# Attention of a decoder layer: heads packed on tiles of the TensorE array, weighted values one group later

## Chip, cores and metric

One core of a Trainium2 chip runs the whole kernel in one launch. The metric is the device time of that launch in microseconds (us). Three runs of the kernel before gave 1297.28, 1297.92 and 1300.14 us; their median is 1297.92 us.

## What is computed

The kernel is one decoder layer with B = 8 sequences of L = 100 tokens and D = 256 features: a two-way Mamba mixer, cross attention to a context of S = 361 tokens, and a mixture of experts. The change is in the cross attention, which is, for every sequence:

```python
q, k, v = heads(x2n @ Wq), heads(ctx @ Wk), heads(ctx @ Wv)   # H = 16 heads of HD = 16 features
p = softmax(q @ k.T / sqrt(HD))        # 100 x 361 for each head
x = x + concat(p @ v) @ Wo + bo
```

All of it is float32. Products of which the operands would be rounded are made of three: high x high, high x low, low x high part.

## The kernel before

Five instruction streams (PE is TensorE, DVE is VectorE, ACT is ScalarE, POOL is GpSimd, SP issues DMAs) run in orders written out by hand and meet at semaphores. The stages follow one another: the mixer (up to about 778 us in the trace), norms and a fusing product, the attention (about 829 to 1060 us), the experts.

In the attention the loop runs over the 8 sequences, and within a sequence over 8 groups of two heads. For group g of sequence b:

- `scores(b, r, g)`, PE: 2 heads x 3 matmuls (through the helper `three`, L1011), each with 128 rows of contraction, 100 columns of stationary queries and 362 moving key columns. So that 128 features can be contracted for a head of 16, POOL spreads the queries (`spread_queries`, L666): in `q_blk` each head has a copy of the 128 features in which all but its own 16 are zero. The scores of a group go to banks 0 and 1, or 2 and 3, of PSUM.
- `maxima`, DVE: the row maxima of both heads (L1626), and their product with -1/sqrt(HD), the tile `shift` (L1629).
- `exponentials`, ACT: two exponentials (L901), each of which also sums its row into `mass` (a second record, ACTIVATION_READ_ACCUMULATOR).
- `turn_probs`, PE: 6 transposes (L1170) into banks 4 and 5. `copy_probs` copies one bank on DVE (L1637) and the other on ACT (L910).
- `weigh_values`, PE: 2 heads x 3 matmuls, where the probabilities are stationary (100 columns) and the 16 value columns of the head move (L1186). The trace has a float32 matmul as two records, so twelve here; a float32r matmul (scores, keys, values) and a transpose are one.

PE's order in `attend` is, for g from 2: `turn_probs(g)`, `scores(g + 2)`, a piece of the next sequence's keys or values (keys with g = 2 and 3, values with g = 4 and 5), `weigh_values(g)`. ACT takes `copy_probs(g)`, `exponentials(g + 2)` and, with g = 2 and 3, the high part of the keys (`high_keys`, L892). DVE takes `copy_probs(g)`, `maxima(g + 2)`, the low part of the keys (`low_keys`, L1613) or the copy of the values. At the end of a sequence DVE divides by the mass (`normalise_heads`), PE transposes the 100x256 result (`turn_heads`), DVE copies it, and PE multiplies with Wo (`project_heads`, 2 matmuls); DVE adds that to `x_tok` (`add_attention`, L1659). Keys, values and the heads' result share the bank KEY_BANK.

Of the kernel before, what the change touches and what calls it, by code (L numbers as in the profile page):

```python
# [18 lines left out]
F32 = mybir.dt.float32  # L19
# [8 lines left out]
P = 128  # L28
B, L, D = 8, 100, 256
T = B * L  # L30
# [52 lines left out]
KEY_BANK = 7  # L83
# [75 lines left out]
def decoder_layer(nc, x, ctxT, winT, wxT, wdtT, woutT, vec, ln_g, ln_b, wfuseT, bfuse,  # L159
                  wqT, wkT, wvT, woT, bo, wg, w1, b1, w2, b2, out):  # L160
    stack = ExitStack()
    with stack:
# [3 lines left out]
        def sem(name):  # L166
# [7 lines left out]
        head_mask = sb("head_mask", [P, HT])  # L174
        one = sb("one", [P, 1])
# [55 lines left out]
        qT_part = [sb(f"qT_{n}", [P, KD, T], F32R, scope=attn) for n in "hl"]  # L231
        q_blk = [[sb(f"q_blk_{n}{r}", [P, KD, HT, L], F32R, scope=attn) for n in "hl"] for r in range(2)]
        ctx_sb = [sb(f"ctx{r}", [P, KD, S], scope=attn) for r in range(2)]
        ctx_part = [[sb(f"ctx_{n}{r}", [P, KD, SE], F32R, scope=attn) for n in "hl"] for r in range(2)]
        wq_sb, wk_sb, wv_sb, wo_sb = (sb(n, [P, KD, D], scope=attn) for n in ("wq_sb", "wk_sb", "wv_sb", "wo_sb"))
        wk_part, wv_part = ([sb(f"{w}_{n}", [P, KD, D], F32R, scope=attn) for n in "hl"] for w in ("wk", "wv"))
        kT_part = [[sb(f"kT_{n}{r}", [P, KD, SE], F32R, scope=attn) for n in "hl"] for r in range(2)]
        v_sb = [sb(f"v{r}", [P, KT, D], scope=attn) for r in range(2)]
        probs = [sb(f"probs{r}", [L, 2, KT * P], scope=attn) for r in range(2)]
        probsT = [[sb(f"probsT{r}{j}", [P, KT * L], scope=attn) for j in range(2)] for r in range(2)]  # L240
        neg_max, shift, mass, inv_mass = (
            sb(n, [L, 2, H], scope=attn) for n in ("neg_max", "shift", "mass", "inv_mass"))
        heads_tok = sb("heads_tok", [L, D], scope=attn)
        headsT = sb("headsT", [P, KD, L], scope=attn)
# [118 lines left out]
        q_blk_ready = sem("q_blk_ready")  # L363
# [10 lines left out]
        shift_ready = sem("shift_ready")  # L374
# [6 lines left out]
        headsT_done = sem("headsT_done")  # L381
# [34 lines left out]
        def tile(k):  # L416
            return slice(k * P, (k + 1) * P)

# [13 lines left out]
        def _(sp):  # L432
# [120 lines left out]
        def _(pool):  # L553
# [21 lines left out]
            fill(head_mask[:], 1.0)  # L575
# [73 lines left out]
            pool.wait_ge(attnw_in, 16 * 4)  # L649
# [10 lines left out]
            def spread_queries(b, r):  # L660

                for m in range(KD):
                    if isinstance(b, int):
                        job_copied(pool, ("qT", m, b // BQ))
                    for part, block in zip(qT_part, q_blk[r]):
                        nc.gpsimd.tensor_tensor(  # L666
                            block[:, m],
                            part[:, m, bass.ds(b * L, L)].bitcast(F32).unsqueeze(1).broadcast_to([P, HT, L]),
# [1218 lines left out]
```

## Time and profile before

| | |
|---|---|
| median of three runs | 1297.92 us |
| the profiled execution | 1293.94 us |
| its span on the core | 1292.2 us |
| PE, DVE, ACT, POOL busy | 80%, 72%, 42%, 61% of the span |
| granted TensorE clock, mean | 0.914 of full speed |
| attention, from the first transposed probabilities to the last add | 846.58 to 1060.27 us |

Busy times are sums of records; matmuls are pipelined, so their records overlap, and the time that one costs is the distance between two starts.

### The profile page before, as it was taken

The numbers are of one execution on the slowest core, as the hardware profiler recorded it, in microseconds if no ns is written. First come the engines' busy times: TensorE is split into PE (matmuls) and PEld (weight loads), VectorE is DVE, ScalarE is ACT, GpSimd is POOL, SyncE is SP. The second block draws the span as 40 slices with busy tenths as digits, with TensorE's granted clock in tenths as the row PEclk, the third lists the DMA queues.
The fourth block names the chain that finished last, engine by engine and source line by source line (L and its number), as shares of the span: only waits on it lengthen the run. The fifth ranks groups of instructions, "written<-read, shape, count | busy, mean of one in ns | idle before, by whom it ended". The sixth has DMA issues, their size and how long they took to land.

```text
span 1292.2 us, 14793 instructions
## 1 busy us (share of the span) xinstructions
PE 1033.0 (80%) x4832; PEld 705.2 (55%) x4832; DVE 925.3 (72%) x1068; ACT 542.0 (42%) x1188; POOL 782.5 (61%) x469
## 2 busy tenths in 40 slices
PE   7596676767667676676765779889999979899996
PEld 5243333433334333343332447779999966499995
DVE  6978998998989989999999993666666652021111
ACT  2686443443444434444444431244444433133231
POOL 4255998998998989989899890555223000402112
PEclk9877888998979989799898999999999988899998
DMA  5001344454544434344454430331000000959995
GB/s 163 1 7 45 98 103 105 94 111 87 110 105 90 108 89 110 105 93 104 94 111 105 96 83 7 115 113 36 13 0 0 0 1 1 331 170 303 319 311 142
DMA packets 95706, 131.70 MB, mean 102 GB/s; under 512 B 12153, under 2 KB 89098, under 8 KB 95626
## 3 DMA queue, kind: packets, MB, share of 16 engines
q1 hardware_dynamic: 91738, 126.59, 36.7%
q0 software_dynamic: 3904, 4.33, 1.8%
q8 instruction: 31, 0.51, 0.2%
q14 instruction: 33, 0.27, 0.1%
HBM read 122.48 MB, written 9.23 MB: 102 GB/s over the span
## 4 chain that ended last, share of the span: by engine, by line
PE 37%; DVE 27%; issue 26%; POOL 5%; ACT 1%; SPq 1%; another core or an unknown queue 1%; DMA 1%; DVEq 0%; POOLq 0%; ACTq 0%
DVE states L1538 13%; DVE states L1550 10%; PE ps L1011 6%; PE ps L1378 6%; PE ps L1392 5%; PE ps L1186 4%; PE ps L1004 3%; PE ps L1170 2%; PE ps L1078 2%; PE ps L1069 2%; PE ps L1315 2%; PE ps L1324 2%; POOL dt L596 1%; POOL dtu L600 1%; POOL row_sel L565 1%
## 5 line engine op out<-in xcount | busy, mean ns | idle before, releaser
L619 POOL TENSOR_TENSOR states<-states,c_row 128x800 f32<-128x800 f32 x255 | 474.4, 1883 | 58.7 <-DVE states L1550 57.7
L1550 DVE TENSOR_TENSOR_SCAN states<-ps,states 128x800 f32<-128x800 f32 x256 | 462.7, 1830 | 0.0
L852 ACT ACTIVATE ps<-dt,neg_a 128x396 f32<-128x396 f32 x512 | 283.4, 585 | 361.8 <-DVE states L1550 361.8
L1078 PE MATMUL ps<-states,ident 128*128 128x400 f32 x1024 | 417.1, 543 | 1.9 <-POOL states L619 1.9
L1078 PEld LDWEIGHTS ps<-states,ident 128*128 128x128 f32 x1024 | 211.2, 210 | 142.0 <-issue 52.4
L1538 DVE TENSOR_TENSOR states<-dtu,ps 128x800 f32<-128x800 f32 x192 | 188.1, 980 | 31.1 <-PE ps L1060 28.3
L1060 PE MATMUL ps<-b_parts,row_sel 96*128 96x400 bf16 x192 | 69.0, 360 | 161.8 <-DVE states L1538 156.3
L1060 PEld LDWEIGHTS ps<-b_parts,row_sel 96*128 96x128 bf16 x192 | 18.9, 99 | 237.6 <-DVE states L1538 220.1
L610 POOL TENSOR_TENSOR states<-dtu,b_row 128x800 f32<-128x800 f32 x64 | 121.1, 1892 | 0.0
L901 ACT ACTIVATE probs<-ps,shift 100x361 f32<-100x361 f32 x128 | 70.8, 559 | 99.1 <-DVE shift L1629 99.1
L740 POOL DMA_INDIRECT sums<-y_tile,x_tile x20 | 30.9, 1546 | 133.7 <-DMA sums<-y_tile,x_tile 92.6
L971 ACT ACTIVATE hid_tile<-ps,w_tile 128x128 f32<-128x128 f32 x160 | 45.6, 368 | 97.8 <-PE ps L1378 97.8
L1186 PEld LDWEIGHTS ps<-v,probsT 128*100 128x100 f32 (+1 forms) x768 | 75.4, 168 | 10.9 <-issue 8.3
L666 POOL TENSOR_TENSOR q_blk_h<-qT_h,head_mask 128x800 fp32r<-128x800 f32 x16 | 24.4, 1524 | 91.2 <-PE ps L1011 81.4
L1186 PE MATMUL ps<-v,probsT 128*100 128x16 f32 (+1 forms) x768 | 74.9, 236 | 5.4 <-ACT probsT L910 4.6
L1378 PEld LDWEIGHTS ps<-x_turned,w_tile 128*128 128x128 f32 x640 | 75.4, 194 | 2.2 <-issue 1.3
L1378 PE MATMUL ps<-x_turned,w_tile 128*128 128x128 f32 x640 | 75.7, 277 | 1.0 <-DVE out_tok L1789 1.0
L1626 DVE TENSOR_REDUCE neg_max<-ps 100x2 f32<-100x722 f32 x64 | 58.1, 908 | 25.5 <-PE ps L1011 25.5
L731 POOL DMA_INDIRECT rows_by_slot<-rows_src,slot_idx x16 | 16.0, 1000 | 99.7 <-DVE slot_idx L1765 95.1
L1392 PE MATMUL ps<-w_tile,hid_tile 128*128 128x256 f32 x320 | 72.2, 379 | 0.0
L1392 PEld LDWEIGHTS ps<-w_tile,hid_tile 128*128 128x128 f32 x320 | 59.3, 190 | 7.3
L994 PE MATMUL ps<-xT,win 128*128 128x400 f32 x128 | 52.8, 579 | 7.4 <-ACT u_pad L753 7.4
(220 smaller groups left out, 1326.4 us busy)
## 6 DMA issues: line engine op xcount, KB each, us to landing
c_row<-rows SPq DMA_DIRECT2D x256, 200.0 KB, 3.1
w_tile<-in_w SPq DMA_DIRECT2D x40, 1024.0 KB, 5.1
b_row<-rows SPq DMA_DIRECT2D x64, 200.0 KB, 4.1
ctx<-in_ctxT SPq DMA_DIRECT2D x8, 361.0 KB, 4.3
rows_by_slot<-blank_rows SPq DMA_DIRECT2D x1, 2660.0 KB, 11.6
x_tile<-rows_by_slot SPq DMA_DIRECT2D x20, 133.0 KB, 3.4
win<-in_winT SPq DMA_DIRECT2D x2, 1024.0 KB, 9.4
w_shared<-in_w SPq DMA_DIRECT2D x2, 1024.0 KB, 6.6
```

The costliest lines, as they stand in the source:

```text
L610: nc.gpsimd.tensor_tensor(states[i % RING][:].rearrange("p (c t) -> p c t", c=CP), dtu[d][:, cp * CP:(cp + 1) * CP, chunk(q)], b_row[turn ...
L619: nc.gpsimd.tensor_tensor(st, st, c_row[i % C_SLOTS][:].unsqueeze(1).broadcast_to([P, CP, TQ]), ALU.mult).then_inc(product_ready, 1)
L852: nc.scalar.activation(seqs(decay[i % DECAYS][:, j * TQ:(j + 1) * TQ])[:, :, 1:], seqs(dt_sb[d][:, c, chunk(q)])[:, :, 1:], ACT.Exp, scale ...
L901: nc.scalar.activation(probs[g % 2][:, j, 0:S], ps[0:L, g % 2 * 2 + j, 0:S], ACT.Exp, bias=shift[:, r, h:h + 1], scale=HD ** -0.5, accum_o ...
L1011: mm = nc.tensor.matmul(to, w[i], x[j], start=(first and n == 0), stop=(last and n == 2))
L1060: nc.tensor.matmul(ps[:, 6 + turn % 2, 0:TQ], row_sel[:, n, :], b_parts[d][:, chunk(q)], start=True, stop=True).then_inc(b_bank_ready, 1)
L1078: mm = nc.tensor.matmul(ps[:, j, 0:TQ], ident[:], states[i % RING][:, j * TQ:(j + 1) * TQ], start=False, stop=(i % N == N - 1), skip_group ...
L1186: mm = nc.tensor.matmul(ps[0:L, 6, h * HD:(h + 1) * HD], probsT[g % 2][j][0:size, kt * L:(kt + 1) * L], v_sb[r][0:size, kt, h * HD:(h + 1) ...
L1378: mm = nc.tensor.matmul(ps[:, hid_bank(k, ft), ft % 4 * P:(ft % 4 + 1) * P], w[:, W1_AT + m * F + ft * P:W1_AT + m * F + (ft + 1) * P], x_ ...
L1392: mm = nc.tensor.matmul(ps[:, 6 + k % 2, 0:D], hid_tile[k % 2][:, ft, :], w[:, W2_AT + ft * D:W2_AT + (ft + 1) * D], start=(ft == 0), stop ...
L1538: nc.vector.tensor_tensor(states[i % RING][:].rearrange("p (c t) -> p c t", c=CP), dtu[d][:, cp * CP:(cp + 1) * CP, chunk(q)], ps[:, bank_ ...
L1550: nc.vector.tensor_tensor_scan(st, decay[i % DECAYS], st, 0.0, ALU.mult, ALU.add).then_inc(scan_done, 1)
```

## The change

Only the attention changes. (1) The 16 features of a head are assigned to a strip of 32 rows of the array (two heads share a strip; a mask keeps only one of them, in `q_part[par]`, and has the factor 1/sqrt(HD) in it). A score matmul contracts 32 rows, and the two heads of a group lie in neighbouring strips, issued in turn. POOL's spreading of the queries is gone; ACT and DVE make two masked copies of the queries instead of one. (2) The value matmuls are turned around: the values of a head, 16 columns, a column of ones and 15 zeros, are stationary (32 columns), the 100 columns of transposed probabilities move, and the results of the two heads go to neighbouring strips of 32 PSUM partitions. The column of ones gives the mass of each row. (3) So ACT no longer sums, DVE no longer makes `shift`, and the 128 x 400 result needs no transpose; a matmul with a selecting matrix spreads the mass, DVE takes the reciprocal of 128 x 400 elements and multiplies, and Wo is applied by 4 matmuls instead of 2, from a `wo_sb` that 8 small DMAs fill. (4) `weigh_values` is issued one group later. (5) PE's loop over the sequences is written out; POOL zeroes the padded tiles before the attention.

```diff
-            fill(head_mask[:], 1.0)
+            fill(head_mask[:], HD ** -0.5)
...
-            for w_dram, w_sbuf in ((wqT, wq_sb), (wkT, wk_sb), (wvT, wv_sb), (woT, wo_sb)):
+            for w_dram, w_sbuf in ((wqT, wq_sb), (wkT, wk_sb), (wvT, wv_sb)):
...
+            sp.wait_ge(wo_zeroed, 1)
+            for m in range(KD):
+                for j in range(P // QUAD):
+                    sp.dma_start(wo_sb[j * QUAD:j * QUAD + HD, m * PAR:(m + 1) * PAR, :],
+                                 woT.rearrange("(m j r i) e -> m j i r e", m=KD, j=P // QUAD, r=PAR)[m, j]
+                                 ).then_inc(wo_in, 16)
...
+            job_result(pool, ("mix", DIRS - 1, B // 2 - 1))
+            nc.gpsimd.memset(wo_sb[:], 0.0).then_inc(wo_zeroed, 1)
+            nc.gpsimd.memset(mass_sel[:], 0.0).then_inc(sel_ready, 1)
+            for r in range(2):
+                nc.gpsimd.memset(v_sb[r][:], 0.0).then_inc(v_zeroed, 1)
...
-            spread_queries(0, 0)
...
-            spread_queries(1, 1)
...
             def high_queries(m, q):
                 job_result(act, ("qT", m, q))
-                nc.scalar.activation(qT_part[0][:, m, chunk(q)], bank(("qT", m, q))[:, 0:TQ], ACT.Copy
-                                     ).then_inc(q_high, 1)
+                for i in range(PAR):
+                    ins = nc.scalar.activation(q_part[i][0][:, m, chunk(q)], bank(("qT", m, q))[:, 0:TQ],
+                                               ACT.Identity, scale=par_mask[:, i:i + 1])
+                ins.then_inc(q_high, 1)
...
                     nc.scalar.activation(probs[g % 2][:, j, 0:S], ps[0:L, g % 2 * 2 + j, 0:S], ACT.Exp,
-                                         bias=shift[:, r, h:h + 1], scale=HD ** -0.5,
-                                         accum_out=mass[:, r, h:h + 1]).then_inc(probs_ready, 1)
+                                         bias=neg_max[:, r, h:h + 1]).then_inc(probs_ready, 1)
...
-                for j in range(2):
-                    mm = three(ps[0:L, g % 2 * 2 + j, 0:SE], [part[:, m, (2 * g + j) % HT, :] for part in q_blk[r]],
-                               [part[:, m, :] for part in kT_part[r]], True, True)
+                for n, (hi, lo) in enumerate(((0, 0), (0, 1), (1, 0))):
+                    for i in range(2):
+                        _, j, par = head_at(2 * g + i)
+                        rows = slice(j * QUAD, (j + 1) * QUAD)
+                        mm = nc.tensor.matmul(ps[0:L, g % 2 * 2 + i, 0:SE],
+                                              q_part[par][hi][rows, m, b * L:(b + 1) * L],
+                                              kT_part[r][lo][rows, m, :], start=(n == 0), stop=(n == 2))
...
-                for j in range(2):
-                    h = 2 * g + j
-                    for kt in range(KT):
-                        size = P if kt < KT - 1 else SL
-                        mm = nc.tensor.matmul(ps[0:L, 6, h * HD:(h + 1) * HD],
-                                              probsT[g % 2][j][0:size, kt * L:(kt + 1) * L],
-                                              v_sb[r][0:size, kt, h * HD:(h + 1) * HD],
+                for kt in range(KT):
+                    size = P if kt < KT - 1 else SL
+                    for i in range(2):
+                        m, j, par = head_at(2 * g + i)
+                        block = (2 * g + i) // (P // QUAD)
+                        mm = nc.tensor.matmul(ps[j * QUAD:(j + 1) * QUAD, HEAD_BANK, block * L:(block + 1) * L],
+                                              v_sb[r][0:size, kt, m * HT + j * PAR + par, :],
+                                              probsT[g % 2][i][0:size, kt * L:(kt + 1) * L],
                                               start=(kt == 0), stop=(kt == KT - 1))
...
-            def turn_heads(b):
+            def spread_mass(b):
                 pe.wait_ge(heads_ready, b + 1)
...
+                nc.tensor.matmul(ps[:, KEY_BANK, 0:BLOCKS * L], mass_sel[:], heads_raw[:].rearrange("p k t -> p (k t)"),
+                                 start=True, stop=True).then_inc(mass_spread, 1)
...
+                for k in range(BLOCKS):
+                    mm = nc.tensor.matmul(ps[0:L, KEY_BANK, 0:D], headsT[:, k, :], wo_sb[:, k, :], start=(k == 0),
+                                          stop=(k == BLOCKS - 1))
...
-                    weigh_values(b, r, g)
+                    weigh_values(b, r, g - 1)
                 if last:
-                    turn_heads(b)
+                    weigh_values(b, r, GROUPS - 1)
+                    spread_mass(b)
                     project_heads(b)
                 else:
                     turn_probs(b + 1, 0)
                     scores(*nxt, 2)
-                    turn_heads(b)
-                    weigh_values(*nxt, 0)
+                    weigh_values(b, r, GROUPS - 1)
                     turn_probs(b + 1, 1)
                     scores(*nxt, 3)
+                    spread_mass(b)
+                    weigh_values(*nxt, 0)
                     project_heads(b)
-                    weigh_values(*nxt, 1)
...
-            with pe.Fori(0, B // 2 - 1) as i:
-                attend(2 * i + 1, 1)
-                attend(2 * i + 2, 0)
+            for b in range(1, B - 1):
+                attend(b, b % 2)
...
                 nc.vector.tensor_reduce(neg_max[:, r, 2 * g:2 * g + 2], ps[0:L, g % 2 * 2:g % 2 * 2 + 2, 0:S],
-                                        AX.X, ALU.max).then_inc(max_ready, 1)
-                dve.wait_ge(max_ready, GROUPS * b + (g + 1))
-                nc.vector.tensor_scalar(shift[:, r, 2 * g:2 * g + 2], neg_max[:, r, 2 * g:2 * g + 2],
-                                        -HD ** -0.5, None, ALU.mult).then_inc(shift_ready, 1)
+                                        AX.X, ALU.max, negate=True).then_inc(max_ready, 1)
...
+            def copy_heads(b):
+                dve.wait_ge(pv_done, GROUPS * b + GROUPS)
+                nc.vector.tensor_copy(heads_raw[:].rearrange("p k t -> p (k t)"), ps[:, HEAD_BANK, 0:BLOCKS * L]
+                                      ).then_inc(heads_ready, 1)
+
+            def normalise_heads(b):
+                dve.wait_ge(mass_spread, b + 1)
+                nc.vector.reciprocal(inv_mass[:].rearrange("p k t -> p (k t)"), ps[:, KEY_BANK, 0:BLOCKS * L]
+                                     ).then_inc(inv_mass_ready, 1)
                 dve.wait_ge(inv_mass_ready, b + 1)
...
+                nc.vector.tensor_tensor(headsT[:], heads_raw[:], inv_mass[:], ALU.mult).then_inc(headsT_copied, 1)
...
-                normalise_heads(b, r)
                 if not last:
                     copy_probs(b + 1, 0)
                     maxima(b + 1, 1 - r, 2)
                 copy_heads(b)
-                if last:
-                    norm_x(0, rows_src)
                 if not last:
                     copy_probs(b + 1, 1)
                     maxima(b + 1, 1 - r, 3)
+                normalise_heads(b)
+                if last:
+                    norm_x(0, rows_src)
                 add_attention(b)
```

## Rows read from the trace of the kernel before

**Rows 1.** Windows: stretch, length, busy (count) of PE, PEld, DVE, ACT, POOL, clock, DMA, GB/s.
```profile
933.40:1038.67 105.27, 103.83 (x914) 99.78 (x913) 64.28 (x128) 52.11 (x168) 23.81 (x16) 1.00 0.00 0
1038.67:1060.27 21.60, 16.80 (x134) 14.36 (x133) 11.85 (x32) 8.35 (x24) 0.00 (x0) 0.84 0.00 1
```

**Rows 2.** Timeline, a group of the last sequence without keys or values: start, length, engine, operation.
```profile
1043.50 0.71 PE L1170 MATMUL ps<-ident,probs 100*128 100x100 f32 x6
...
1043.99 0.39 PE L1011 MATMUL ps<-kT_h,q_blk_h 128*100 128x362 f32 x1
...
1044.25 0.47 DVE L1637 COPY probsT<-ps 128x300 f32<-128x300 f32 x1 [0.96 <-PE ps L1170]
...
1044.41 0.42 ACT L910 ACTIVATE probsT<-ps 128x300 f32<-128x300 f32 x1
...
1044.88 0.32 PE L1011 MATMUL ps<-kT_h,q_blk_l 128*100 128x362 f32 x1
1045.04 1.15 PE L1186 MATMUL ps<-v,probsT 128*100 128x16 f32 x12
1045.24 0.91 DVE L1626 TENSOR_REDUCE neg_max<-ps 100x2 f32<-100x722 f32 x1 [0.52 <-PE ps L1011]
1046.04 0.71 PE L1170 MATMUL ps<-ident,probs 100*128 100x100 f32 x6
...
1046.39 0.56 ACT L901 ACTIVATE probs<-ps,shift 100x361 f32<-100x361 f32 x1 [1.56 <-DVE shift L1629]
...
1047.48 0.42 ACT L910 ACTIVATE probsT<-ps 128x300 f32<-128x300 f32 x1
...
1062.47 0.88 ACT L753 ACTIVATE xn3T<-ps 128x400 f32<-128x400 f32 x2
```

**Rows 3.** Timeline, a group with keys (g = 3) and the values that follow.
```profile
911.07 0.46 DVE L1637 COPY probsT<-ps 128x300 f32<-128x300 f32 x1
911.45 0.90 DVE L1626 TENSOR_REDUCE neg_max<-ps 100x2 f32<-100x722 f32 x1
...
912.59 0.56 ACT L901 ACTIVATE probs<-ps,shift 100x361 f32<-100x361 f32 x1 [1.65 <-DVE shift L1629]
...
913.68 0.47 ACT L892 ACTIVATE kT_h<-ps 128x362 fp32r<-128x362 f32 x1
...
914.18 0.53 DVE L1613 TENSOR_TENSOR kT_l<-ps,kT_h 128x362 fp32r<-128x362 f32 x1 [1.62 <-ACT kT_h L892]
...
914.63 0.46 DVE L1637 COPY probsT<-ps 128x300 f32<-128x300 f32 x1
...
914.86 0.29 PE L1011 MATMUL ps<-wv_h,ctx_h 128*128 128x256 f32 x1
...
916.29 1.15 PE L1186 MATMUL ps<-v,probsT 128*100 128x16 f32 x12
```

**Rows 4.** Timeline, PE alone: 8 float32 matmuls with 9 stationary and 100 moving columns.
```profile
1109.59 1.54 PE L1302 MATMUL ps<-ident,rows_src 100*9 100x100 f32 x16
```

**Rows 5.** Groups of DVE instructions, shapes apart: busy us, mean ns.
```profile
L1641 DVE RECIPROCAL inv_mass<-mass 100x16 f32<-100x16 f32 x8 | 1.9, 243 | 0.0
L1445 DVE RECIPROCAL rstd<-std 100x4 f32<-100x4 f32 x10 | 1.8, 178 | 7.7 <-ACT std L749 7.7
...
L1456 DVE COPY xn2T<-ps 128x400 f32<-128x400 f32 x2 | 1.0, 564 | 0.0
```

**Rows 6.** Timeline, the start of the attention.
```profile
839.95 3.66 DVE L1629 TENSOR_SCALAR shift<-neg_max 100x2 f32<-100x2 f32 x1
...
846.58 0.70 PE L1170 MATMUL ps<-ident,probs 100*128 100x100 f32 x6 [3.18 <-DVE qT_l L1604]
...
853.39 0.47 DVE L1637 COPY probsT<-ps 128x300 f32<-128x300 f32 x1 [1.42 <-PE ps L1170]
```

**Rows 7.** Windows of one microsecond, columns as in rows 1.
```profile
845.00:846.00 1.00, 0.00 (x0) 0.00 (x0) 0.73 (x2) 0.63 (x2) 1.00 (x2) 1.00 0.00 0
...
1054.00:1055.00 1.00, 0.55 (x4) 0.44 (x3) 0.34 (x1) 0.10 (x1) 0.00 (x0) 0.50 0.00 0
```

More of the change, by code:

```diff
@@ L82 @@
 ROUTE_CONSTS = 13
-KEY_BANK = 7
+KEY_BANK, HEAD_BANK = 7, 6
+QUAD = 32
+PAR = QUAD // HD
+BLOCKS = H // (P // QUAD)
+HEAD_CONSTS = 7
 FIRST_KEYS, FIRST_VALUES = (0, 1), (4, 5)
@@ L417, in tile, with head_at @@
             return slice(k * P, (k + 1) * P)
+        def head_at(pos):
+            m, rest = divmod(pos, HT)
+            par, j = divmod(rest, P // QUAD)
+            return m, j, par
         def hid_bank(k, ft):
@@ L647, in split_context @@
                 split_into([part[:, :, 0:S] for part in ctx_part[r]], ctx_sb[r][:], ctx_split, 2 * b)
-            pool.wait_ge(attnw_in, 16 * 4)
+            job_result(pool, ("mix", DIRS - 1, B // 2 - 1))
[3 more added lines that the diff above has]
+                nc.gpsimd.memset(v_sb[r][:], 0.0).then_inc(v_zeroed, 1)
+            pool.wait_ge(sel_ready, 1)
+            selected = mass_sel[:].rearrange("p (j i) -> p j i", i=QUAD)
+            nc.gpsimd.affine_select(out=selected, in_=selected, compare_op=ALU.not_equal, fill=1.0, base=-HD,
+                                    pattern=[[-QUAD, P // QUAD], [0, QUAD]], channel_multiplier=1
+                                    ).then_inc(sel_ready, 1)
+            pool.wait_ge(v_zeroed, 2)
+            for r in range(2):
+                nc.gpsimd.memset(v_sb[r][:, :, :, HD:HD + 1], 1.0).then_inc(v_zeroed, 1)
+            pool.wait_ge(attnw_in, 16 * 3)
             for n, (part, raw) in enumerate(((wk_part, wk_sb), (wv_part, wv_sb))):
@@ L659, in _ @@
                 nc.gpsimd.memset(probs[r][:, :, S:], 0.0).then_inc(probs_zeroed, 1)
[L660 to L668, printed above, removed]
-                            head_mask[:].unsqueeze(2).broadcast_to([P, HT, L]), ALU.mult).then_inc(q_blk_ready, 1)
-            spread_queries(0, 0)
             pool.wait_ge(xn_ready, (1 + DIRS + 1) * B)
@@ L1603, in low_queries @@
                 dve.wait_ge(q_high, q * KD + m + 1)
-                nc.vector.tensor_tensor(qT_part[1][:, m, chunk(q)], bank(("qT", m, q))[:, 0:TQ],
-                                        qT_part[0][:, m, chunk(q)].bitcast(F32), ALU.subtract
-                                        ).then_inc(copied["v"], 1)
+                for i in range(PAR):
+                    ins = nc.vector.scalar_tensor_tensor(
+                        q_part[i][1][:, m, chunk(q)], bank(("qT", m, q))[:, 0:TQ], par_mask[:, i:i + 1],
+                        q_part[i][0][:, m, chunk(q)].bitcast(F32), ALU.mult, ALU.subtract)
+                ins.then_inc(copied["v"], 1)
+            dve.wait_ge(mask_ready, 1)
             for m in range(KD):
@@ L1689, in _ @@
             maxima(0, 0, 1)
+            dve.wait_ge(v_zeroed, 4)
             for part in range(2):
```

73 lines of the change are left out of this document (30 added, 43 removed).

## Prediction, written before the changed kernel had run

> **What bounds the kernel now.** I read the page's forty slices first, which put the attention apart as the stretch where PE is full, then the windows over that stretch. Over four sequences PE is busy 103.8 of 105.3 us at full clock, ACT half and DVE 61% of it [rows 1]. One sequence takes 105.27 / 4 = 26.3 us. So PE has no slack, but what it would run into next must be read from the timeline, and there are two such chains.
>
> In a group without keys PE's turn starts at 1043.50 and again at 1046.04: 2.54 us, made of 0.49 for six transposes, 1.05 for six score matmuls and 1.00 for twelve value records [rows 2]. In a group with keys the reader should follow DVE and ACT instead: copy, maxima, two exponentials, high keys, low keys, next copy, each right behind the other: 914.63 - 911.07 = 3.56 us [rows 3]. That is a closed chain through two engines which wait for each other in fixed order. PE merely happens to need the same time there. Whatever PE saves with g = 2 and 3 is lost again unless this chain shrinks too.
>
> **The parts.**
>
> *Scores.* Six matmuls, 0.16 us from one start to the next, now in three pairs on different rows of the array. Unit price 3 x 0.165 = 0.49 us if the members of a pair run side by side, 6 x 0.165 = 0.98 if not. No row shows two matmuls side by side. Records of neighbours overlap (0.32 us long, 0.16 apart [rows 2]), which is the pipeline only. I take 0.49: the two share no rows of the array, no bank and no stationary data. Both ends are kept.
>
> *Values.* Now 32 stationary and 100 moving columns. The nearest row has 9 stationary and 100 moving columns: (1.54 - 0.25) / 15 = 0.086 us for a record [rows 4], where 0.25 is the length of the last. Twelve make 1.03 us, as much as now; the turn around alone buys nothing. The two records of a matmul need the same strip, so they follow one another, while the second can run beside the first of the other head: seven slots instead of twelve, 0.58 us. I take 0.58, ends 0.58 and 1.03. The Trainium skill ("TensorE: Matmul & The Clock Gate", section Measured speedup vs the span model) gives 2.38 times for three column strips; by that rule the pairs overlap, without it I would be at the first rival. No run so far shows it.
>
> *Changes between kinds of tile.* Turn to scores, scores to values or keys, values to turn: three or four in each group. Lower end: what a change between kinds of matmul costs today, 1.05 - 6 x 0.165 = 0.06 us. Upper end: the array has to empty first, the length of a matmul beyond its pitch, 0.32 - 0.16 = 0.16 us [rows 2]. Nothing is nearer to one end; I take 0.12. The skill ("TensorEngine Tiling (Array Packing)", section Key Properties) says that changing the mode drains the engine; by that the price is the upper end and the sum further down becomes 1289 instead of 1282.
>
> *Maxima and exponentials.* `shift` goes: from the start of the maxima to the exponential were 1.15 us, now 0.91 + 0.03. Two exponentials with their sums took 1.09 us until ACT's next operation (1046.39 to 1047.48 [rows 2]). Without the second record the nearest pair is two copies of 400 columns in 0.88 us, of which the last is 0.50: pitch 0.38 [rows 2]. I take 0.82 until ACT goes on, 0.90 until the probabilities are there. The chain of a group with keys becomes 0.38 + 0.94 + 0.82 + 0.50 + 0.45 = 3.09 us instead of 3.56. PE needs there 0.49 + 0.49 + 1.0 (keys) + 0.58 + 4 x 0.12 = 3.04: the chain sets it.
>
> *The end of a sequence.* Removed: two transposes, a copy, a small reciprocal. Added: a copy of 128x400 (0.56 us [rows 5]), the mass matmul (two records of 400 columns, at 0.86 ns a column and record 0.34 each: 0.67 us), a reciprocal of 400 columns, a multiply (0.57), and four matmuls with Wo, eight records of 256 columns at 0.216 = 1.73 us, twice as much as now. The reciprocal is the unknown: 178 ns at 4 columns, 243 at 16 [rows 5], so 5.4 ns a column and, at 400, about 2.2 us. Lower end 0.6 us, if the slope of so short rows were not a price for each column. I take 2.2, because it is the only slope of this operation.
>
> *POOL and SP.* Spreading is removed. Nobody waits for it in steady state; it costs something at the start only. The zeroing is done before the keys' weights arrive, while POOL waits for them; without this cover it would be some 5 us. Eight small DMAs for `wo_sb` start before the context's data are used and are needed 45 us later: nothing. SP has no other work in that stretch. The written-out loop changes no order: nothing. ACT and DVE make the queries twice, 4 more operations of 0.5 to 0.6 us each.
>
> **One sequence, in order.** Zero is DVE's copy with g = 2, 0.75 us after the start of its turn (1043.50, 1044.25 [rows 2]). Maxima start 0.36 after the start of the last score matmul (1044.88, 1045.24).
> - Groups 2 and 3: copies at 0, 3.26, 6.35. The values of the next sequence wait for the low keys, until 6.53.
> - Group 4: values 1.43 us (914.86 to 916.29 [rows 3]), then 0.12 + 0.58 + 0.12, turn at 8.78, copy at 9.53. Group 5: 0.49 + 0.12 + 0.49 + 0.12, half as many values 0.71, 0.82 for the weighing: turn at 11.53.
> - Groups 6, 7, 0' and 1' (the next sequence's): 0.49 + 0.49 + 0.58 + 3 x 0.12 = 1.92 each, turns at 13.45, 15.37, 17.29. The chain over two groups (0.75 + 1.46 to the end of the maxima, then exponentials 0.85, ACT's copy 0.42, wait 0.14) gives 1.81 a group, just below.
> - End: scores at 17.90, last one at 18.23, maxima 18.59 to 19.50, reciprocal to 21.74, multiply to 22.35, Wo 22.45 to 24.18, then the turn with g = 2, its copy at 24.93. PE has done the mass and the first weighing by 19.88 and stands 2.6 us: the stall that was hidden in PE's order now sits behind the reciprocal, and `turn_probs` of g = 2 is late next.
>
> So 24.9 us instead of 26.3: 1.4 saved, seven times, 10 us. The delay of `weigh_values` itself is worth little: it takes away PE's waits for ACT's copy, 1.5 of 105 us at most [rows 1].
>
> **Start.** `shift` stood 3.66 us [rows 6] beside POOL's addition to `x_tok`; a normal one takes 0.17. It held back the exponentials, the queries' second half and so PE, which waited 3.18 us. With it and the spreading gone, and about 1.0 us more for the doubled query copies, the first turn comes some 2.8 us earlier. From it to the first copy with g = 2 were 6.81 us; 1.36 until the second turn, exponentials and ACT's copy until 3.48, turn at 3.6 and copy at 4.35 save 2.4. Together 5 us.
>
> **Last sequence.** Six groups without keys save 6 x (2.54 - 1.92) = 3.7 of 21.6 us [rows 1]. The end has copy, mass, reciprocal and multiply in line, 4.0 us, where about 1.3 stood. The norm behind them hides the longer Wo. 1 us saved.
>
> **Sum.** 10 + 5 + 1 = 16 us of the profiled 1293.94; that lies 4 us below the median, so I take the difference to the median: 1297.9 - 16 = 1282 us. With 0.06 for a change of tile a sequence is 24.0 us and the total 1274, with 0.16 it is 25.8 and 1289; with the short reciprocal another 11 us less.
>
> **Rivals.**
> 1. *Value pairs do not run side by side.* 1.03 instead of 0.58 in the six groups which PE sets: +2.7 us a sequence, 27.6 in all, 1.3 longer than now; with what start and end give, 1303 us (1293 to 1311 by the tile change). For it: each matmul is two records with their own loads, and all moving columns must reach strips in the same 128 rows. 18%.
> 2. *Slower: neither kind overlaps.* Scores 0.98 too, 8 x 0.49 more: 31.5 us a sequence, 7 x 5.2 = 36 longer, 1331 us (1315 to 1345). It decides as soon as a pair takes over about 0.25 us in the scores and 0.17 in the values. PE is full today, so nothing absorbs it. 12%.
> 3. *The clock.* PE's pause of 2.6 us recurs with each sequence. Granted clock stayed at 1.00 in the empty microsecond at 845, yet is 0.50 (1.2 GHz) at 1054, behind a stretch with PE busy in part [rows 7]. If it falls each time, turn, scores and keys take twice as long, 2 us, of which the chain hides a little: +1.7 x 7, 1294 us, up to 1310. 10%.
> 4. *PE alone counts.* If the reciprocal costs 0.6 and tile changes 0.06, a sequence takes 22.4 us: 1262. 10%.
>
> **Chances and range.** My forecast has 50%, own range 1270 to 1292. The range reaches from the fourth rival to the middle of the first, 1262 to 1307, and leaves out the second. What this kernel's measurement tells from no change is 0.2%, 2.6 us. Faster: 50 + 10, half of the third, a little of the first, 67%. Same 8%. Slower 25%.
>
> **What would show it.** Pairs of score records starting within hundredths of a microsecond, and the stretch of six near 0.5; twelve value records in 0.58 or 1.03 us; the gap from the last score to the first record of another kind; copies of g = 2 and 3 3.1 us apart; the reciprocal near 2.2 us with a PE pause before Wo. The prediction is wrong if value records come one by one, if the reciprocal is short, or if the clock falls at the end of each sequence.

## The result, and the profile after

The changed kernel takes 1312.94 us (median of four runs, 1308.74 to 1316.47) against 1298.87 us of the kernel before beside it: a ratio of 1.011, 95% interval 1.0088 to 1.0132. It is slower, by some 14 us; 1282 us and "faster" had been predicted, and 1307 was the upper end of the range. The profiled execution took 1308.74 us, its span is 1307.0 us, and the mean granted clock 0.898 (0.914 before).

Windows of the kernel after, columns as in [rows 1]. The first stretch is four sequences, from DVE's copy with g = 2 to the same copy four sequences later; the second is the last sequence.

```profile
939.53:1055.55 116.02, 105.15 (x930) 77.10 (x932) 67.61 (x97) 47.69 (x104) 5.96 (x4) 0.88 0.00 1
1055.55:1075.71 20.16, 15.48 (x152) 10.48 (x153) 14.12 (x28) 7.62 (x16) 0.00 (x0) 0.92 0.00 1
```

Four sequences took 105.27 us before [rows 1] and take 116.02 now. PE is no longer full (105.15 of 116.02), and its clock, 1.00 before, is 0.88. The last sequence is shorter: 20.16 us against 21.60.

The group without keys is as short as it was meant to be. Timeline of the kernel after, one such group; it answers to [rows 2].

```profile
953.49 0.73 PE L1191 MATMUL ps<-ident,probs 100*128 100x100 f32 x6
953.99 1.01 ACT L919 ACTIVATE probs<-ps,neg_max 100x361 f32<-100x361 f32 x2 [1.28 <-DVE neg_max L1655]
954.16 0.41 PE L1179 MATMUL ps<-kT_h,q_h 32*100 32x362 f32 x2
954.26 0.47 DVE L1663 COPY probsT<-ps 128x300 f32<-128x300 f32 x1 [0.39 <-PE ps L1191]
954.40 0.32 PE L1179 MATMUL ps<-kT_l,q_h 32*100 32x362 f32 x2
954.57 0.32 PE L1179 MATMUL ps<-kT_h,q_l 32*100 32x362 f32 x2
954.82 0.71 PE L1208 MATMUL ps<-probsT,v 128*32 128x100 f32 x12
...
955.46 0.73 PE L1191 MATMUL ps<-ident,probs 100*128 100x100 f32 x6
```

Turn to turn is 1.97 us instead of 2.54. The score records come in pairs that share one row (x2, together 0.32 us long, as long as a single one in [rows 2]), and from the first pair to the values pass 0.66 us; the values take 0.64 until the next turn. The same timeline has the group with keys, which answers to [rows 3]:

```profile
943.01 0.46 DVE L1663 COPY probsT<-ps 128x300 f32<-128x300 f32 x1
...
943.38 0.90 DVE L1655 TENSOR_REDUCE neg_max<-ps 100x2 f32<-100x722 f32 x1
...
944.32 1.02 ACT L919 ACTIVATE probs<-ps,neg_max 100x361 f32<-100x361 f32 x2 [1.20 <-DVE neg_max L1655]
...
945.22 0.47 ACT L910 ACTIVATE kT_h<-ps 128x362 fp32r<-128x362 f32 x1
945.73 0.53 DVE L1640 TENSOR_TENSOR kT_l<-ps,kT_h 128x362 fp32r<-128x362 f32 x1 [1.44 <-ACT kT_h L910]
...
946.18 0.46 DVE L1663 COPY probsT<-ps 128x300 f32<-128x300 f32 x1
```

3.17 us a group instead of 3.56. What eats this and more stands at the end of each sequence:

```profile
930.72 0.46 DVE L1663 COPY probsT<-ps 128x300 f32<-128x300 f32 x1
...
931.27 0.94 PE L1216 MATMUL ps<-heads_raw,mass_sel 128*128 128x400 f32 x2
931.38 0.91 DVE L1655 TENSOR_REDUCE neg_max<-ps 100x2 f32<-100x722 f32 x1 [0.20 <-PE ps L1179]
932.14 0.71 PE L1208 MATMUL ps<-probsT,v 128*32 128x100 f32 x12
932.25 2.66 DVE L1672 RECIPROCAL inv_mass<-ps 128x400 f32<-128x400 f32 x1
...
934.94 0.58 DVE L1675 TENSOR_TENSOR headsT<-heads_raw,inv_mass 128x400 f32<-128x400 f32 x1
935.57 3.41 PE L1224 MATMUL ps<-wo_sb,headsT 128*100 128x256 f32 x8 [2.72 <-DVE headsT L1675]
938.82 0.68 PE L1191 MATMUL ps<-ident,probs 100*128 100x100 f32 x6
...
939.53 0.47 DVE L1663 COPY probsT<-ps 128x300 f32<-128x300 f32 x1
```

PE waits 2.72 us for the reciprocal and the multiply, and then Wo takes 3.25 us until the turn, where eight records at 0.216 would take 1.73. From copy to copy are 8.81 us; 6.89 were predicted. The windows say why (columns as in [rows 1]):

```profile
934.00:935.00 1.00, 0.00 (x0) 0.00 (x0) 0.96 (x2) 0.00 (x0) 0.00 (x0) 1.00 0.00 0
935.00:936.00 1.00, 0.43 (x1) 0.41 (x2) 0.52 (x1) 0.00 (x0) 0.00 (x0) 0.55 0.00 0
936.00:937.00 1.00, 1.00 (x4) 0.61 (x3) 0.00 (x0) 0.00 (x0) 0.00 (x0) 0.50 0.00 0
937.00:938.00 1.00, 1.00 (x4) 0.73 (x3) 0.00 (x0) 0.00 (x0) 0.00 (x0) 0.50 0.00 0
938.00:939.00 1.00, 1.00 (x7) 0.72 (x6) 0.00 (x0) 0.00 (x0) 0.00 (x0) 0.74 0.00 0
```

The granted clock is 0.50 (1.2 GHz) while PE works on Wo behind its pause. That pause stands once in each of the seven sequences, and the clock fell behind it all seven times in this trace. In every other sequence it falls a little earlier and stays at 0.50 longer (905 to 914, for instance), into the first group with keys, which then takes 5.3 us instead of 3.48. So the copies with g = 2, at 852.35, 881.60, 910.00, 939.53, 967.93, 997.53, 1025.85 and 1055.55, are 28.3 and 29.5 us apart in turn, 29.03 on average, against 26.47 before.

At the start the gain is 1.0 us where 5 were predicted: the first copy with g = 2 stands at 852.35 instead of 853.39 [rows 6]. Timeline of the kernel after, at the start of the fusing product:

```profile
806.87 2.70 POOL L673 MEMSET v<- 128x1536 f32 x2
...
808.36 1.23 DVE L1464 TENSOR_SCALAR var_eps<-moments 100x4 f32<-100x4 f32 x1
...
811.51 3.12 PE L1004 MATMUL ps<-flip,mix_tok 100*128 100x100 f32 x16 [2.58 <-DVE mix_tok L1469]
...
814.43 16.27 PE L1021 MATMUL ps<-wfuse_sb,xT 128*100 128x256 f32 x64
```

The small `var_eps` takes 1.23 us beside POOL's zeroing (0.17 elsewhere), PE waits 2.58 us (1.52 before), and the product runs 16.27 us (14.68 before), as the clock is at 0.50 from 813 to 819 where it was there from 812 to 814 before. The queries start at 832.07 instead of 829.27, and the 3 us that the missing `shift` gives back are gone before the attention begins.

The balance of the two profiled spans: start -1.0, seven sequences 7 x (29.03 - 26.47) = +17.9, last sequence -1.4, the rest behind it -0.6; together +14.9 us, and 1307.0 - 1292.2 = 14.8.

### The profile page after: what moved, and what is told of

It is laid out like the page before. It is cut to its first block, busy times and chain, and to the rows that moved or that the text cites. A ratio compares the mean times of both kernels' runs of the same rounds, so it can differ in the third digit from the quotient of the medians.

```text
span 1307.0 us, 14434 instructions
## 1 busy us (share of the span) xinstructions
PE 1029.6 (79%) x4864; PEld 657.6 (50%) x4864; DVE 929.2 (71%) x1009; ACT 535.2 (41%) x1064; POOL 740.0 (57%) x444
## 4 chain that ended last, share of the span: by engine, by line
PE 36%; DVE 28%; issue 26%; POOL 6%; DMA 2%; SPq 1%; ACT 0%; DVEq 0%; POOLq 0%; ACTq 0%
DVE states L1562 13%; DVE states L1574 10%; PE ps L1400 6%; PE ps L1414 5%; PE ps L1179 3%; PE ps L1021 3%; PE ps L1191 3%; PE ps L1028 3%; PE ps L1208 3%; PE ps L1095 2%; PE ps L1224 2%; PE ps L1086 2%; DVE inv_mass L1672 2%; POOL dt L616 1%; POOL dtu L620 1%
## 5 line engine op out<-in xcount | busy, mean ns | idle before, releaser
L919 ACT ACTIVATE probs<-ps,neg_max 100x361 f32<-100x361 f32 x128 | 64.9, 559 | 61.4 <-DVE neg_max L1655 61.4
L657 POOL TENSOR_TENSOR ctx_h<-ctx,one 128x722 fp32r<-128x722 f32 x8 | 11.1, 1390 | 119.7 <-PE ps L1028 107.0
L1826 DVE COPY x_turned<-ps 128x256 f32<-128x256 f32 x20 | 8.5, 425 | 67.1 <-PE ps L1388 67.1
L927 ACT ACTIVATE probsT<-ps 128x300 f32<-128x300 f32 x64 | 26.9, 420 | 65.6 <-PE ps L1191 65.6
```

What stands on the lines that cost most here:

```text
L919: nc.scalar.activation(probs[g % 2][:, j, 0:S], ps[0:L, g % 2 * 2 + j, 0:S], ACT.Exp, bias=neg_max[:, r, h:h + 1]).then_inc(probs_ready, 1)
```

## The experiments

Ratios are to the kernel before, run on the same chip (medians 1298.69, 1298.57 and 1299.09 us in the three sets), with 95% intervals. A sequence is measured between DVE's copies with g = 2, over all seven or, where the text says so, over the last six, which leave out the slow clock at the start.

| run | us | ratio |
|---|---|---|
| warm, 14 matmuls before Wo | 1293.05 | 0.9956 (0.9939 to 0.9973) |
| Wo one group later | 1278.97 | 0.9864 (0.9832 to 0.9896) |
| no reciprocal | 1270.60 | 0.9781 (0.9765 to 0.9797) |
| head by head | 1314.20 | 1.0096 (1.0061 to 1.0132) |
| Wo later, both heads on one strip | 1338.98 | 1.0325 (1.0299 to 1.0352) |
| values at once, 12 matmuls | 1306.16 | 1.0069 (1.0044 to 1.0095) |
| Wo later, zeroing on DVE | 1282.62 | 0.9880 (0.9857 to 0.9903) |
| before, without `shift` | 1286.81 | 0.9922 (0.9902 to 0.9943) |
| warm, 10 matmuls before Wo | 1287.65 | 0.9920 (0.9900 to 0.9941) |
| Wo later, 10 matmuls at the start | 1275.84 | 0.9840 (0.9818 to 0.9862) |
| the same, zeroing on DVE | 1276.63 | 0.9829 (0.9808 to 0.9850) |
| Wo later, again | 1281.38 | 0.9871 (0.9850 to 0.9892) |

**The clock.** Matmuls of 112 columns into a place that nobody reads fill PE's pause, first fourteen, later ten; the output stays as it is.

```diff
                     weigh_values(*nxt, 0)
+                    keep_warm(14)
                     project_heads(b)
```

> The changed kernel with 14 extra matmuls (identity with 112 columns, into unused columns of the heads' bank, 28 records of some 0.09 us) on PE between the first weighing of the next sequence and Wo, where PE stands 2.7 us while DVE takes the reciprocal. They do nothing for the result and do not shorten the chain. Theory (the pause lets the clock fall): granted clock stays at 1.00, Wo takes 1.7 to 1.9 us instead of 3.4 to 3.7, a sequence 26 us instead of 29.0, the total falls by some 21 us to about 1292. Rival (the narrow tiles let it fall, or something outside PE): the clock is still 0.50 during Wo, the total stays at 1308 to 1316.

> The changed kernel with ten instead of fourteen matmuls ahead of Wo into columns that nobody reads. With fourteen, the last of them ended 0.5 us after the operand of Wo was there (958.24 against 957.75), so a sequence of 26.45 us holds some 0.5 us of their own; ten take 2.4 us and end before. Expected if the clock stays up: 25.95 us a sequence, 7 x 0.5 = 3.5 us below the run with fourteen (1293.05), 1289 to 1290 us. This is then the change without the clock's fall, to be set against the 24.9 us a sequence of the prediction. Rival (ten leave a pause in which the clock falls again): above 1300 us.

Fourteen gave 1293.05 us; ten gave 1287.65. In both traces the clock is at 1.00 from 860 us to the last sequence; before that it is at 0.50 for some 7 to 10 us behind the pause at the start, as in the kernel after (849 to 857). Timeline and windows of the run with ten:

```profile
900.40 2.66 DVE L1678 RECIPROCAL inv_mass<-ps 128x400 f32<-128x400 f32 x1
...
900.93 2.48 PE L1230 MATMUL ps<-mass_sel,ident 128*128 128x112 f32 x20
...
903.72 1.97 PE L1224 MATMUL ps<-wo_sb,headsT 128*100 128x256 f32 x8 [0.30 <-DVE headsT L1681]
905.53 0.68 PE L1191 MATMUL ps<-ident,probs 100*128 100x100 f32 x6
...
906.54 0.47 DVE L1669 COPY probsT<-ps 128x300 f32<-128x300 f32 x1 [0.22 <-issue]
```

```profile
902.00:904.00 2.00, 1.70 (x14) 1.49 (x14) 1.63 (x2) 0.00 (x0) 0.00 (x0) 1.00 0.00 0
904.00:906.00 2.00, 2.00 (x14) 1.62 (x12) 0.10 (x1) 0.00 (x0) 0.00 (x0) 1.00 0.00 0
```

Wo is as late behind the reciprocal as before (903.72 - 900.40 = 3.32), but it takes 1.81 us until the turn instead of 3.25. From the first copy with g = 2 (852.51) to the last (1036.69) are 26.31 us a sequence against 29.03. So the fall of the clock costs 2.7 us a sequence, 19 us in seven: more than the loss of 14, and shown, since nothing differs but the matmuls that fill the pause. Without it the change would be worth 11 us, not 16.

**Where the end of a sequence waits.** Two edits: a copy in place of the reciprocal (the heads are then multiplied by the mass instead of divided), and Wo moved behind the next group's work, with DVE's addition moved likewise (and DVE's loop over the sequences written out for it). The first leaves out the division, so what it computes is not the attention; it serves the timing alone.

```diff
-                nc.vector.reciprocal(inv_mass[:]..., ps[:, KEY_BANK, 0:BLOCKS * L]
+                nc.vector.tensor_copy(inv_mass[:]..., ps[:, KEY_BANK, 0:BLOCKS * L]
```

> The changed kernel, with a copy in the place of the reciprocal of 128x400, so the heads are multiplied with their mass instead of divided by it. Theory (reciprocal of 2.66 us, and the pause that it makes): 0.56 instead of 2.66 us, the pause shrinks to 0.6 us, the clock stays at 1.00 with the tiles unchanged: a sequence 29.0 - 2.1 - 3 = 23.9 us, total 1274 to 1280. Rival (tiles themselves lower the clock): only the 2.1 us a sequence come back, total about 1297, clock 0.50 in parts of each sequence.

```diff
                     weigh_values(*nxt, 0)
-                    project_heads(b)
...
                         scores(b, r, g + 2)
...
+                    if g == 2 and b:
+                        weigh_values(b, r, 1)
+                        project_heads(b - 1)
```

> The changed kernel, but Wo of a sequence is issued one group later, behind the next sequence's turn, scores and weighing of g = 2 and before its keys; DVE adds it behind the maxima of that group. Theory (what costs is that PE's whole queue waits behind the reciprocal): PE has 1.6 us of work more in the pause, the rest of the pause is some 1 us, the clock stays at 1.00 and g = 2 no longer waits for Wo: 24.5 to 26 us a sequence, total 1275 to 1290. Rival (DVE's order holds g = 2 back anyway, as its copy stands behind reciprocal and multiply): ACT's copy is early, DVE's is not, PE still pauses over 2 us, the clock still falls: total above 1300.

Without the reciprocal: 1270.60 us. Timeline of that run:

```profile
947.07 0.57 DVE L1672 COPY inv_mass<-ps 128x400 f32<-128x400 f32 x1
...
948.31 1.97 PE L1224 MATMUL ps<-wo_sb,headsT 128*100 128x256 f32 x8 [0.64 <-DVE headsT L1675]
950.12 0.68 PE L1191 MATMUL ps<-ident,probs 100*128 100x100 f32 x6
```

The pause is 0.64 us and the clock stays at 1.00. 42 us lie between this run and the change (36.7 between the profiled spans). 19 of them are the clock's by the run above, and some 15 the reciprocal's own: the last six sequences take 23.99 us each, against 26.09 in the run with ten matmuls. With Wo later the reciprocal has work beside it: 1278.97 us, and 1281.38 when the same kernel ran again. A sequence is 24.86 us in the last six and 24.97 over all seven, the pause before Wo 0.75 us in that trace, the clock 1.00 from 860 us on. This one beats both kernels and does all of the work.

**Do the pairs run side by side?** First the order of issue: all three matmuls of one head before the other head's, in the scores and in the values.

```diff
-                for n, (hi, lo) in enumerate(((0, 0), (0, 1), (1, 0))):
-                    for i in range(2):
+                for i in range(2):
+                    for n, (hi, lo) in enumerate(((0, 0), (0, 1), (1, 0))):
```

> The changed kernel, with the six score matmuls and the six value matmuls of a group issued head by head instead of in turn, so that only the seam between the two heads lies on two strips. Theory (pairs run side by side because they are issued in turn): scores 5 x 0.165 = 0.83 instead of 0.49 us, values 11 x 0.086 = 0.95 instead of 0.5, a plain group 2.7 instead of 1.97 us, so 3 to 5 us a sequence more in the groups which PE sets: total 1330 to 1345. Rival (the hardware looks far ahead, or a plain group is set by DVE and ACT): within 5 us of the changed kernel, 1308 to 1318.

```profile
954.60 0.41 PE L1179 MATMUL ps<-kT_h,q_h 32*100 32x362 f32 x2
...
954.85 0.33 PE L1179 MATMUL ps<-kT_l,q_h 32*100 32x362 f32 x2
955.01 0.33 PE L1179 MATMUL ps<-kT_h,q_l 32*100 32x362 f32 x2
955.27 0.91 PE L1208 MATMUL ps<-probsT,v 128*32 128x100 f32 x12
...
956.11 0.73 PE L1191 MATMUL ps<-ident,probs 100*128 100x100 f32 x6
```

The expectation failed: 1314.20 us, no different from the change. The scores take 0.67 us as before: by the records the second head's first matmul starts beside the first head's, although two others were issued between them. Only the values pay, 0.84 us instead of 0.64. These groups are 0.2 us longer and the whole is not, since the ends are shorter (7.4 to 8.3 us where the change has 8.7 to 9.7). Windows of this run, columns as in [rows 1], say why:

```profile
903.00:911.00 8.00, 5.48 (x42) 3.70 (x40) 5.20 (x7) 2.33 (x6) 0.00 (x0) 1.00 0.00 0
1054.00:1073.00 19.00, 19.00 (x121) 14.34 (x119) 6.41 (x10) 6.16 (x13) 0.00 (x0) 0.50 0.00 0
```

PE pauses 2.52 us before Wo in each of the seven sequences, but the clock fell behind three of these pauses only (at 937, 995 and 1053). Behind the other four, as at 905.55 to 908.07 in the first window, Wo took its full-clock 1.80 us until the turn. The third fall lasted 20 us with PE full and made the last sequence 8 us longer than in the change. So the equal times say nothing of the order of issue: in this trace longer groups stand against fewer falls. Nor can it tell whether two strips are what makes the pairs cheap. The next run does, by giving both heads of a group the same strip; the values are head by head in it, which costs the 0.2 us just seen.

```diff
-            par, j = divmod(rest, P // QUAD)
+            j, par = divmod(rest, PAR)
```

> The kernel with Wo one group later (1278.97 us), with the heads of a pair taken from one strip of 32 rows instead of two, and its value matmuls issued head by head. Nothing else differs. If running side by side is what makes the pairs cheap, six score records cost 6 x 0.165 = 0.98 us instead of 0.50 and twelve value records about 1.03 instead of 0.6; a plain group goes from 1.97 to about 2.8 us. The keys' groups stay with their chain at 3.2. Over a sequence some 4 to 5 us more in the groups which PE sets: 1310 to 1320 us. Rival (the pairs are cheap because the records are small, not because two strips work at once): plain groups stay at 1.97 us and the time at 1279, or 1285 if only the order of the values counts.

```profile
964.84 0.57 PE L1179 MATMUL ps<-kT_h,q_h 32*100 32x362 f32 x2
...
965.25 0.48 PE L1179 MATMUL ps<-kT_l,q_h 32*100 32x362 f32 x2
965.58 0.49 PE L1179 MATMUL ps<-kT_h,q_l 32*100 32x362 f32 x2
966.00 0.37 PE L1028 MATMUL ps<-wv_h,ctx_h 128*105 128x256 f32 x1
```

Now the members of a pair start one after the other (the row of two is 0.57 us long instead of 0.41); the six take 1.16 us to the next kind instead of 0.66, a group without keys 2.98 us instead of 1.97, and the run 1338.98 us, 60 more than with two strips. The groups with keys grew too (3.7 and 4.6 us), which the expectation had left with their chain. The strips' overlap is real. Of the 60 us the order of the values explains some 13 (an estimate, 64 groups at 0.2 us); the rest is more than any other edit here moved.

**The delay of the values.** Each group's values in its own group again, with twelve matmuls before Wo to keep the clock. Wo keeps its place. The mass and DVE's copy of the heads move one group ahead, so they come inside the last two groups, and the weighing of the next sequence's group 1 comes behind Wo.

```diff
-                    weigh_values(b, r, g - 1)
+                    weigh_values(b, r, g)
```

> The changed kernel with each group's weighted values issued in their own group again, as the kernel before does, and with twelve matmuls into an unused bank column range ahead of Wo, so that the clock should stay up; its neighbour is the changed kernel with fourteen such matmuls (1293.05 us), which keeps the values one group later. My theory of the prediction: the delay itself buys little, at most PE's waits for ACT's copy, some 0.1 to 0.2 us in each group that PE sets: 1293 to 1300 us. Rival (the delay is what makes the short groups possible, since PE now has fewer records to cover the copies of the transposes with): a plain group grows from 1.97 to over 2.3 us, a sequence by 3 us, the total to about 1315 us.

1306.16 us, between the two expectations. A group without keys takes 1.98 us, exactly as with the delay (1.97), which the first theory had. The last two take 2.68 and 2.75 instead of 2.06 and 1.89, and the end 8.1 to 8.2 instead of 7.7 to 8.0: 28.3 us a sequence against 26.4 with fourteen matmuls (the last six of each). The delay is worth nothing inside the groups. At the end the mass and two weighings stand ahead of the reciprocal and behind Wo instead of beside DVE's work, which costs 1.9 us a sequence in this arrangement; whether another order of the undelayed values would do better was not tried.

**The start, and `shift` alone.** In the kernel with Wo later, DVE zeroes `v` behind its early small operations, in POOL's place.

```diff
-                nc.gpsimd.memset(v_sb[r][:], 0.0).then_inc(v_zeroed, 1)
+                nc.vector.memset(v_sb[r][:], 0.0).then_inc(v_zeroed, 1)
```

> The kernel with Wo one group later (1278.97 us), with the zeroing of v taken from POOL's start and given to DVE after its early small operations, behind which it waits anyhow. Theory: POOL's two memsets (2.70 us each) hold back DVE's small addition of epsilon (1.23 us instead of 0.17) and with it TensorE's first transposes and its clock, and this puts the queries 2.8 us later; without them the epsilon addition is back near 0.17 us, the queries start near 829 instead of 832, and the total falls by 2 to 3 us, to 1276. Rival: the lateness comes from elsewhere (the longer loads or the rest of the start), or is absorbed before the first copy of group 2: total within 0.7 us of 1279.

1282.62 us: no gain. (The two memsets take 2.70 us together, not each.) Its trace has the local effect: `var_eps` 0.17 us, the queries at 828.66 instead of 831.13, the first copy with g = 2 at 849.32 instead of 852.49 (against the first run with Wo later). One sequence later 1.0 us is left of these 3.2, as the clock was at 0.50 for longer. So ten matmuls were put into PE's pause of 2.6 us before the first turn, without and with that zeroing, beside the kernel with Wo later.

```diff
             pe.wait_ge(v_copied, 2)
+            keep_warm(10)
```

> The kernel with Wo one group later (1278.97 us), with ten matmuls that nobody reads between the last queries and the first turn, where TensorE stands 2.6 us (843.6 to 846.2) and then runs at a granted clock of 0.50 for 10 us (847 to 857). If the pause is what makes it fall, the clock stays at 1.00 and the stretch from the first turn to the third copy shrinks by 2 to 4 us: 1275 to 1277 us. Rival (the fall comes from the mix of busy and idle time before the pause, or from the work behind it): clock 0.50 again and the time within 1 us of the kernel with Wo later.

> Both: the zeroing of v on DVE and the ten matmuls in the pause at the start. Alone, the zeroing brought the first copy of group 2 3.2 us forward (849.32 against 852.49), but the granted clock was then 0.50 from 846 to 859 and only 1.0 us of it was left one sequence later. If the clock ate the rest, with the clock kept up all 3 us stay: 2 to 3 us less than the run with the ten matmuls alone, 1272 to 1275 us. Rival (the gain is lost to another wait, such as the context's load or its split): no difference from the run with the matmuls alone.

> The kernel with Wo one group later, unchanged, on the same chip as the two runs with matmuls in the start's pause, as their neighbour: 1277 to 1282 us.

Windows of the kernel with Wo later (first fence) and of the same with ten matmuls (second):

```profile
848.00:850.00 2.00, 2.00 (x13) 1.29 (x13) 1.03 (x3) 1.32 (x3) 0.00 (x0) 0.50 1.08 348
855.00:857.00 2.00, 2.00 (x17) 1.31 (x17) 0.54 (x1) 0.90 (x2) 0.00 (x0) 0.50 1.05 332
```

```profile
848.00:850.00 2.00, 1.63 (x22) 1.02 (x20) 1.88 (x3) 1.34 (x4) 0.00 (x0) 1.00 1.07 351
855.00:857.00 2.00, 2.00 (x24) 1.57 (x22) 0.61 (x1) 1.36 (x3) 0.00 (x0) 1.00 1.12 277
```

Filling the pause kept the clock up here too. But a pause of this length does not take it down each time. In the kernel before PE stood 3.18 us at this place ([rows 6]) and the clock stayed at 1.00 behind it, from 846 to 864 us; with the values at once it stood 2.58 us and the clock stayed at 1.00 as well, and the run head by head had four such cases. What decides it no run here shows. The third sequence's copy with g = 2 stands at 902.71, 899.14 and 897.01 us: 3.6 us for the clock, 2.1 more for the zeroing once the clock stays up. The medians are 1281.38, 1275.84 and 1276.63; their intervals overlap, so the whole time does not resolve the zeroing's 2 us. Runs of one kernel here spread by some 5 us.

Last, one part of the change alone in the kernel before: the factor in the mask, the maxima negated by their own instruction, no `shift`; the sums stay.

```diff
-                                        AX.X, ALU.max).then_inc(max_ready, 1)
-                nc.vector.tensor_scalar(shift[:, r, 2 * g:2 * g + 2], ...
+                                        AX.X, ALU.max, negate=True).then_inc(max_ready, 1)
```

> The kernel before with one part of the change alone: 1/sqrt(HD) goes into the head mask, the maxima are negated by their own instruction, and the small multiplication to shift is gone. Theory: PE sets the plain groups of the kernel before, and the keys' chain is as long as PE's own work, so nothing is gained in steady state beyond 0.2 us a sequence; at the start the 3.66 us operation is gone and the first copy of group 2 comes some 2 us earlier. Total 1294 to 1297 us against 1298.7. Rival (the chain through the small operation sets the sequence): 8 x 0.25 us a sequence, 16 us in all, about 1283 us.

1286.81 us, 12 us better at the median, and neither theory. The start gives 1.6 us, and a sequence 25.83 us instead of 26.47. The group of DVE instructions in question, in the kernel before, from the first copy with g = 2 to the end of the attention (count | busy us, mean ns | idle us):

```profile
L1629 DVE TENSOR_SCALAR shift<-neg_max 100x2 f32<-100x2 f32 x60 | 16.7, 279 | 2.1
```

It takes 279 ns on average where an undisturbed one takes 170; beside POOL's spreading of the queries single ones took 0.65 and 0.37. Such an operation ends with POOL's product: 972.92 + 0.65 = 973.57, where the product that began at 972.02 ran 1.52 us, to 973.54. So the prediction's "Nobody waits for it in steady state" holds for semaphores only; three groups in most sequences were held up by it or by the context's split. 1.6 + 7 x 0.64 = 6.1 of the 8.7 us between the profiled spans are explained by this; the rest lies behind the seventh sequence and was not pursued.

## Why the prediction was wrong

The reading of before was right: PE full, the chain through DVE and ACT just below it. Most prices held:

- *Scores* at 0.49 and *values* at 0.58 with running side by side as the likelier case: right, 0.66 and 0.64 with their changes of tile, and the run on one strip shows the cause. Rivals 1 and 2 did not occur.
- *Changes between kinds of tile* at 0.12: the group of 1.97 us less 0.49 + 0.49 + 0.58 leaves 0.41 for three, 0.14 each, if those three prices are right. The Trainium skill ("TensorEngine Tiling (Array Packing)", section Key Properties) says that changing the mode drains the engine; the prediction's price for that was 0.16, and the row is between the two.
- *Maxima and exponentials*, the chain at 3.09: 3.17. The last sequence, -1: measured -1.4.
- *Reciprocal* at 2.2 (its two rows give 2.3, as 178 ns stand at 4 columns already): 2.66 us, 6.6 ns a column. The wait before Wo, 2.6, was 2.72.

**The step that failed** is the end of a sequence, taken at full clock against the third rival, *the clock*. The forecast took the end of a sequence, 2.6 us of pause and Wo at 1.73, at full clock, and gave 10% to the clock falling there each time, although [rows 7] showed it at 0.50 behind a stretch of partial work. It fell in every sequence. The rival was also priced too low: +1.7 us a sequence, against 2.7 measured. Wo itself, straight behind the pause, was not in its list of what takes twice as long, and Wo alone lost 3.25 - 1.81 = 1.4 us; in every other sequence the keys were hit as well. With 19 instead of 12 us the rival's own sum would have been 1301 us; the terms that follow add 9 for the sequences and 4 for the start, 1314 in all, where 1312.94 was measured.

**Terms that were mis-sized.** In the run with ten matmuls a sequence takes 26.31 us (26.09 in the last six, all at full clock) and not 24.9, so the ten us of the sequences shrink to 7 x (26.47 - 26.31) = 1.1. In the sequence of the run with ten matmuls from 880.18 to 906.54 us (26.36), the seven copies up to the end take 18.69 us where the prediction had 18.04: each group but the last is 0.05 to 0.2 longer. The end takes 7.67 instead of 6.89 (7.4 in most sequences): 0.46 of it is the reciprocal, 0.1 the Wo matmuls, 0.26 the copy that comes later behind its turn, where DVE adds the heads' result (905.90) ahead of it. *Start*, 5 us: 1.0. That POOL's zeroing is hidden because POOL has time was the wrong question; DVE's small operation was held up by it, and behind PE's pauses there and before the first turn the clock fell. With the zeroing moved and the clock held the first copy with g = 2 stands at 848.70, 4.7 us ahead of the kernel before: the term itself was sound, and what took it away was POOL's zeroing and the clock.

The statement that the stall "now sits behind the reciprocal" and that `turn_probs` of g = 2 is late next was right, and it named the cure: Wo one group later makes the forecast's 24.9 us (24.86 in the last six) and, by 1279 to 1281 us, its total. That agreement is no support for the forecast, since that kernel differs from the one forecast.

The granted clock was still 1.00 in the pause, from 934 to 935, and 0.55 and 0.50 behind it. The Trainium skill ("TensorE: Matmul & The Clock Gate", section Part 1: The HAM clock gate) says that the clock follows how busy PE has lately been. These traces agree in that filling the pause held the clock in all sixteen places where it was tried (seven each with fourteen and ten matmuls, two at the start); they also have pauses of 2.52 and 3.18 us without a fall.

## What to carry to other kernels

When a change makes PE faster, ask where PE will now stand idle and what it does next: a pause of 2.7 us that recurs cost on average another 2.7 us through the half clock behind it, and that price falls on the instructions straight after the pause. Put work there (an order in which the waiting matmul comes one group later), or, cheaper to write, a few matmuls that nobody reads; ten of them gave back 25 us by the medians, 21 by the profiled spans. A small DVE operation on the critical path should not run beside long POOL work, be it arithmetic or zeroing.

## What the runs showed of the hardware that was not expected

- A score matmul on a neighbouring strip starts beside one issued three places ahead of it, and before the two between them (954.60, two records in one row, with the heads issued one after the other). With both heads on one strip six took 1.16 us, as without overlap.
- The clock's low stretch lasts well beyond the pause with PE fully busy: 847 to 857 us in the kernel with Wo later, 846 to 859 when the same work starts 2.5 us earlier, 1053 to 1073 in the run head by head. A pause of 2.52 us was followed by a fall three times of seven there, one of 2.72 us seven times of seven in the kernel after, and one of 3.18 us not at all in the kernel before.
- POOL's memsets of 128x1536 hold up a DVE operation of 100x4 elements, 1.23 instead of 0.17 us, and POOL's addition of 100x2048 one of 100x2 (`shift`, 3.66 us in [rows 6]). Both small operations end with POOL's: 839.95 + 3.66 = 843.61, where the addition of 4.55 us that began at 839.04 ends at 843.59.
- A reciprocal of 128x400 from PSUM takes 2.66 us, the copy of the same tile 0.57.
